# TensorE matmuls into an unused bank during the scatters and the norms of the expert stages

## The chip, the core and the metric

The kernel is one program on one NeuronCore of a Trainium2 chip. The core has a matrix engine (TensorE, PE in the rows), a vector engine (VectorE, DVE), a scalar engine (ScalarE, ACT), a general engine (GpSimd, POOL) and SyncE (SP), which here only starts DMA transfers. Each engine works through its own instructions in order, and they signal each other with semaphores. The metric is the device time of one execution in microseconds, the median over several runs. TensorE's clock has two levels here, 1.2 GHz and 2.4 GHz; the profile gives the granted clock as a share of the higher one, 0.50 or 1.00 (a mean over the stretch asked for).

## What is computed

Six layers on x of shape (2, 1024, 128), that is N = 2048 tokens of 128 numbers, everything in fp32. The layers are, cut from the reference:

```
x = x + 0.5 * L0_ffn(layernorm(x))    # 8 experts, at most N/8 = 256 tokens each, relu
x = x + L0_attn(layernorm(x))         # gated linear attention, 16 heads of 8, a scan over time
x = x + 0.5 * L0_ffn(layernorm(x))
x = x + 0.5 * L1_ffn(layernorm(x))    # 8 experts, no limit, hidden width 512, gelu
x = x + L1_attn(layernorm(x))         # softmax attention, its own norm inside
x = x + 0.5 * L1_ffn(layernorm(x))
```

An expert layer picks for each token the expert with the largest router logit, runs that expert's two matrices on the token (128 to 128 to 128 in L0, 128 to 512 to 128 in L1), and scales the result with the router's probability.

## The kernel before

Tokens lie in 16 tiles of 128 (T = 16), x stays in SBUF as X. The stages run in the order of the layers, with ln the number of the norm and k that of the expert stage: FFN0 (ln 0, k 0), linear attention (ln 1), FFN0 (ln 2, k 1), FFN1 (ln 3, k 2), softmax attention (ln 4), FFN1 (ln 5, k 3). The work of each engine is written out by hand, one function for each engine, and every dependence is a wait on a semaphore. There is no scheduler.

A norm works in four chunks of four tiles. VectorE adds the result of the stage before to X, one instruction a tile (line 1086, semaphore x_updated), takes statistics, and writes the normed tiles to XN (line 1042, xn_ready). TensorE transposes the four tiles of a chunk into PSUM bank 0 or 1 (line 554), and ScalarE copies them to XNT (line 883). Behind the transposes of chunk c TensorE computes the router's logits of chunk c-1 (line 536, tiny matmuls of 128x8) or, in the linear stage, the gates (line 543), and the last chunk's at the end. VectorE turns the logits into expert numbers and slots, and waits for that on logits_done. After an FFN0 stage the results come back by 16 gathers of GpSimd (line 1409), one a tile; after an FFN1 stage by four loads of SyncE.

An expert stage begins with two small bf16 matmuls that count tokens (lines 568 and 569, PSUM bank 3). When VectorE has the slots, GpSimd writes the 16 tiles to DRAM in slot order by 16 indirect DMAs (line 1395), all of which add to one semaphore, scattered. SyncE waits for all 16 and then loads the slots back (line 453), four tiles a load. TensorE transposes them group by group (turn, line 581), and ScalarE copies the transposed groups (line 894). In FFN0 each of 8 experts has an up matmul (line 593), ScalarE's relu, and two down matmuls (line 601). The third group's transposes stand ahead of the first expert's up. In FFN1 there are 23 tiles; each has four up matmuls (line 629), a bias on VectorE, gelu on ScalarE (line 928) and four down matmuls (line 640), and ScalarE copies each tile's W1 in front (line 917). TensorE's order there is up(0), up(1), down(0), up(2), down(1) and so on.

The other lines that the text names: 678 values of the linear stage; 699 its output projection, 8 matmuls a batch; 722 the q and k projections of softmax attention, 726 its values, 16 matmuls; ScalarE's table load of line 933 stands ahead of the gates' sigmoid. An fp32 matmul shows as two records in the trace; a transpose as one.

Of the kernel before, what the change touches and what calls it, by code (L numbers as in the profile page):

```python
# [16 lines left out]
P = 128  # L17
B, S = 2, 1024
N = B * S
T = N // P  # L20
# [122 lines left out]
def macaron_kernel(nc, x_in, params, f1_pack, f1_b2, out):  # L143
    with ExitStack() as ctx:
# [3 lines left out]
        def sem(name):  # L148
            return ctx.enter_context(nc.semaphore(name))
# [159 lines left out]
        gath_ready = sem("gath_ready")  # L309
        owner_ready = sem("owner_ready")  # L310
        xg_ready = sem("xg_ready")
        scattered = sem("scattered")
        xs_loaded = [sem(f"xs_loaded{k}") for k in range(6)]
        xs_turned = sem("xs_turned")
        xs_copied = sem("xs_copied")
# [9 lines left out]
        x_updated = sem("x_updated")  # L325
# [106 lines left out]
        def _(sp):  # L432
# [14 lines left out]

            def moe(kind, k):

                sp.wait_ge(scattered, 16 * T * (k + 1))  # L450
                for c, (a, b) in enumerate(chunks_of(kind)):
                    width = P if kind == "ffn0" else P + 1
                    sp.dma_start(XS[:, a:b, 0:width], sx_rows[k][:, a:b, :]).then_inc(xs_loaded[c], 16)
                if kind == "ffn0":
                    for e in range(E):

                        sp.wait_ge(eo_copied, before(k, E, NT) + e + 1)
                        sp.dma_start(sy_rows[:, 2 * e:2 * e + 2, :], EO[:, 2 * e:2 * e + 2, :]).then_inc(eo_stored, 16)
                    return

                sp.wait_ge(y_scattered, 16 * NT * (k - 1))
                for c in range(T // 4):
                    sp.dma_start(YG[:, 4 * c:4 * c + 4, :], ty_rows[:, 4 * c:4 * c + 4, :]).then_inc(y_loaded[c], 16)
# [62 lines left out]
        def _(pe):  # L526
            ident = col("ident")

            def norm_turned(ln, kind):

                wr = col("f0_wr" if kind == "ffn0" else "f1_wr")
# [14 lines left out]
                if ln == 5:  # L546

                    pe.wait_ge(z_scaled, GR)
                for c in range(T // 4):
                    pe.wait_ge(xn_ready, T * ln + 4 * c + 4)  # L550
                    if 4 * ln + c >= 2:
                        pe.wait_ge(xt_copied, 4 * ln + c - 1)
                    for t in range(4 * c, 4 * c + 4):
                        i = nc.tensor.transpose(PS[:, c % 2, (t % 4) * P:(t % 4 + 1) * P], XN[:, t, 0:P], ident)  # L554
                    i.then_inc(xt_turned, 1)
                    if kind in ("ffn0", "ffn1") and c >= 1:
                        logits(c - 1)
                    if kind == "lin" and c >= 1:
                        gates(c - 1)
# [5 lines left out]
            def moe(kind, ln, k):  # L565
# [9 lines left out]
                def turn(c):  # L575
                    a, b = chunks[c]
                    pe.wait_ge(xs_loaded[c], 16 * (k + 1 if c < 4 else k - 1))
                    if c >= 2:
                        pe.wait_ge(xs_copied, nb + c - 1)
                    for t in range(a, b):  # L580
                        i = nc.tensor.transpose(PS[:, c % 2, (t - a) * P:(t - a + 1) * P], XS[:, t, 0:P], ident)  # L581
                    i.then_inc(xs_turned, 1)

                base = before(k, E, NT)
                if kind == "ffn0":
# [800 lines left out]
        def _(pool):  # L1386
            def moe(kind, k):
# [4 lines left out]
                for t in range(T):  # L1392
                    if kind == "ffn0":
                        pool.wait_ge(xg_ready, T * k + t + 1)
                    pool.indirect_dma_start(sx[k], bass.IndirectOffsetOnAxis(ap=SCATI[:, t:t + 1], axis=0),  # L1395
                                            src[:, t, :], None, bounds_check=slots - 1, oob_is_err=False
                                            ).then_inc(scattered, 16)
                if kind == "ffn1":

                    for i in range(NT):  # L1400
# [131 lines left out]
```

## Time and profile before

| | us |
|---|---|
| median of 3 runs | 989.38 |
| lowest and highest | 987.41, 995.13 |
| span of the profiled execution | 985.3 |
| TensorE busy in it | 675.3 (69%) |
| VectorE busy | 582.2 (59%) |
| ScalarE busy | 443.7 (45%) |
| GpSimd busy | 302.9 (31%) |
| mean granted TensorE clock | 0.834 |

The span is from the first to the last instruction. The rows of the next section but one come from this execution. A row of the timeline merges like instructions that follow each other: its start, the time to the end of the last, the engine, the line, the operation with its operands, the count, and in brackets how long the engine had been idle before it and what ended that. "SPq" is SyncE's issuing of DMAs. Busy time of TensorE is not work at its peak, since a matmul at half clock is busy for twice as long.

### The profile page before, as it was taken

The page shows a single profiled execution, that of the slowest core. Times are in us where ns is not written, and L with a number is a line of the kernel's source. Part 1 is how long each engine was busy: PE and PEld are TensorE (multiplying, and loading weights), DVE is VectorE, ACT ScalarE, POOL GpSimd, SP SyncE. Part 2 cuts the span into 40 slices and gives each one's busy share as a digit, 9 for nine tenths or more (in the row PEclk, how much of TensorE's full clock was granted, in tenths as well). Part 3 has the DMA queues.
Part 4 walks back from the last instruction along what each step waited for, and adds up shares of the span by engine and source line. Part 5 has one row for each costly group of instructions (what it writes and reads, how often), then busy time and mean ns, then how long its engine had stood idle before and what let it go on. Part 6 is the DMA issues. An engine that isn't in the chain of part 4 may idle for free.

```text
span 985.3 us, 13757 instructions
## 1 busy us (share of the span) xinstructions
PE 675.3 (69%) x4446; PEld 334.1 (34%) x4446; DVE 582.2 (59%) x1035; ACT 443.7 (45%) x836; POOL 302.9 (31%) x679
## 2 busy tenths in 40 slices
PE   4042867332240992579999999999999999840694
PEld 4031322131230991213343423242323433230693
DVE  5216699760450345677878777767977777062243
ACT  2021500011210652405878676766667777720462
POOL 0605154414425341003242323141322323105242
PEclk9996889555655896757999999998999999965697
DMA  9942000002213101560030202030020000000203
GB/s 232 274 144 40 1 1 0 0 9 60 71 17 90 30 27 44 123 147 7 1 50 2 50 1 50 1 48 4 11 40 2 1 2 1 1 1 33 81 26 96
DMA packets 45926, 44.89 MB, mean 46 GB/s; under 512 B 5904, under 2 KB 36316, under 8 KB 45600
## 3 DMA queue, kind: packets, MB, share of 16 engines
q1 hardware_dynamic: 41168, 35.90, 15.6%
q0 software_dynamic: 4544, 7.60, 2.9%
q8 instruction: 37, 0.61, 0.3%
q10 hardware_dynamic: 144, 0.51, 0.2%
q14 instruction: 33, 0.27, 0.1%
HBM read 27.85 MB, written 17.60 MB: 46 GB/s over the span
## 4 chain that ended last, share of the span: by engine, by line
PE 51%; DVE 11%; issue 5%; DMA 5%; POOL 5%; ACT 3%; SPq 1%; POOLq 0%; ACTq 0%; DVEq 0%
PE PS L828 14%; PE PS L795 12%; PE PS L770 11%; PE PS L629 5%; PE PS L640 4%; POOL slots_x L1395 3%; DVE ARENA L1348 3%; ACT ARENA L987 2%; DMA ARENA<-slots_x 1%; POOL ARENA L1409 1%; DVE XN L1042 1%; PE PS L536 1%; DMA ARENA<-k_parts 1%; DVE STATS L1019 1%; DVE X L1086 1%
## 5 line engine op out<-in xcount | busy, mean ns | idle before, releaser
L1348 DVE TENSOR_REDUCE ARENA<-PS 128x1 f32<-128x1024 f32 x256 | 302.9, 1219 | 94.6 <-PE PS L770 94.1
L987 ACT ACTIVATE ARENA<-PS 128x512 f32<-128x512 f32 x512 | 279.6, 597 | 95.6 <-PE PS L795 89.2
L795 PE MATMUL PS<-ARENA 75*128 75x512 bf16 x512 | 174.9, 388 | 8.3 <-ACT ARENA L987 6.8
L770 PE MATMUL PS<-ARENA 72*128 72x512 bf16 x512 | 164.3, 406 | 21.3 <-DMA ARENA<-k_parts 16.9
L828 PE MATMUL PS<-ARENA 128*8 128x128 f32 (+8 forms) x1920 | 153.4, 435 | 0.7 <-ACT ARENA L987 0.7
L1460 POOL TENSOR_SCALAR_AFFINE_SELECT ARENA<-ARENA 128x128 f32<-128x128 f32 x256 | 74.6, 296 | 160.5 <-ACT ARENA L987 160.3
L581 PE MATMUL PS<-C,ARENA 128*128 128x128 f32 x78 | 17.1, 368 | 119.5 <-DMA ARENA<-slots_x 119.5
L1272 DVE TENSOR_TENSOR ARENA<-PS,ARENA 128x512 f32<-128x512 f32 x46 | 31.8, 692 | 96.3 <-PE PS L629 96.3
L554 PE MATMUL PS<-C,XN 128*128 128x128 f32 x96 | 24.1, 401 | 92.4 <-DVE XN L1042 88.8
L795 PEld LDWEIGHTS PS<-ARENA 75*128 75x128 bf16 x512 | 47.5, 98 | 105.5 <-ACT ARENA L987 56.5
L770 PEld LDWEIGHTS PS<-ARENA 72*128 72x128 bf16 x512 | 44.8, 100 | 104.1 <-issue 37.3
L894 ACT COPY ARENA<-PS 128x512 f32<-128x512 f32 (+1 forms) x20 | 11.5, 573 | 133.5 <-PE PS L581 133.5
L828 PEld LDWEIGHTS PS<-ARENA 128*32 128x32 f32 (+2 forms) x1920 | 43.7, 98 | 76.0 <-issue 38.7
L1402 POOL DMA_INDIRECT tokens_y<-ARENA x46 | 44.7, 972 | 75.3 <-DVE ARENA L1281 74.3
L1450 POOL CAST ARENA<-ARENA 128x4 bf16<-128x4 f32 x64 | 12.1, 190 | 174.6 <-DVE ARENA L1348 174.5
L1420 POOL TENSOR_TENSOR ARENA<-ARENA 128x1024 f32<-128x1024 f32 x16 | 40.3, 2522 | 55.4 <-DVE ARENA L1318 55.4
L629 PE MATMUL PS<-ARENA 128*128 128x128 f32 x368 | 53.6, 293 | 1.2 <-ACT ARENA L917 0.6
L581 PEld LDWEIGHTS PS<-C,ARENA 128*128 128x128 f32 x78 | 12.2, 188 | 122.8 <-issue 119.2
L640 PE MATMUL PS<-ARENA 128*128 x368 | 51.6, 284 | 1.5 <-ACT ARENA L928 1.5
L1318 DVE TENSOR_TENSOR_SCAN ARENA<-ARENA 128x1024 f32<-128x1024 f32 x16 | 51.8, 3245 | 0.0
L1395 POOL DMA_INDIRECT slots_x<-ARENA,SCATI x32 | 31.4, 983 | 64.5 <-DVE ARENA L1222 56.0
L678 PE MATMUL PS<-XNT,C 128*128 128x512 f32 x64 | 37.3, 725 | 18.2 <-DVE ARENA L1304 18.2
(130 smaller groups left out, 785.0 us busy)
## 6 DMA issues: line engine op xcount, KB each, us to landing
ARENA<-q_parts SPq DMA_DIRECT2D x24, 192.0 KB
ARENA<-k_parts SPq DMA_DIRECT2D x72, 64.0 KB
ARENA<-pack_dram SPq DMA_DIRECT2D x8, 514.0 KB
slots_x<-FILL SPq DMA_DIRECT2D x2, 1483.5 KB, 19.0
ARENA<-slots_x SPq DMA_DIRECT2D x10, 258.0 KB, 4.4
ARENA<-slots_x SPq DMA_DIRECT2D x8, 256.0 KB, 3.6
slots_y<-ARENA SPq DMA_DIRECT2D x16, 128.0 KB, 1.8
ARENA<-tokens_y SPq DMA_DIRECT2D x8, 256.0 KB, 3.7
```

Of the source, the lines that this page charges most:

```text
L629: ins = nc.tensor.matmul(PS[:, 4 + i % 2, f * P:(f + 1) * P], W1[:, i % 2, f * P:(f + 1) * P], XST[:, i * P:(i + 1) * P], start=True, stop ...
L640: ins = nc.tensor.matmul(o, HG[:, i % 2, f * P:(f + 1) * P], WT[:, bass.ds(owner[i] * WB + F1 + f * P, P)], start=(f == 0), stop=(f == FB ...
L770: ins = nc.tensor.matmul(PS[:, slot + c, :], Q3[0:KQ, G % Q3R, g, i * P:(i + 1) * P], K3[0:KQ, G % Q3R, g, c * 512:(c + 1) * 512], start=T ...
L795: nc.tensor.matmul(PS[:, bank, 0:w], K3[0:MR + 3, G % Q3R, i, j * P:(j + 1) * P], Q3[0:MR + 3, G % Q3R, i, half * 512:half * 512 + w], sta ...
L828: ins = nc.tensor.matmul(PS[32 * g:32 * g + width, 7, lo:hi], v, probs, start=(what == "denominator" and st in (0, TB)), stop=(j == TB - 1 ...
L987: nc.scalar.activation(PT[:, n % NPT, 0:w], PS[:, 4 + ring_number[x] % NBB, 0:w], ACT.Exp).then_inc(b_exp, 1)
L1318: nc.vector.tensor_tensor_scan(ST[:, n % 2, :], GT[:, b * S:(b + 1) * S], KV[:, n % 2, :], 0.0, ALU.mult, ALU.add).then_inc(state_done, 1)
L1348: nc.vector.tensor_reduce(NM[:, k % 4, i:i + 1], PS[:, slot:slot + 2, :].rearrange("p b n -> p (b n)"), AX.X, ALU.max, negate=True).then_i ...
L1395: pool.indirect_dma_start(sx[k], bass.IndirectOffsetOnAxis(ap=SCATI[:, t:t + 1], axis=0), src[:, t, :], None, bounds_check=slots - 1, oob_ ...
L1402: pool.indirect_dma_start(ty, bass.IndirectOffsetOnAxis(ap=XS[:, i, P:P + 1].bitcast(U32), axis=0), EO[:, i, :], None, bounds_check=N - 1, ...
L1420: nc.gpsimd.tensor_tensor(QS[:, n % 8, :], QT[:, b * S:(b + 1) * S], ST[:, n % 2, :], ALU.mult).then_inc(qs_done, 1)
L1460: nc.gpsimd.affine_select(out=MD[:, n % NPT, :], in_=PT[:, n % NPT, diag:diag + P], compare_op=ALU.is_ge, fill=0.0, base=0, pattern=[[-1, P]],
```

## The change

TensorE gets a function, keep_busy(times), that multiplies the identity by itself into PSUM bank 3, columns 0 to 127, and whose result nobody reads. It is called at two kinds of places. In all four expert stages, behind the counting matmuls and ahead of the transposes, TensorE waits for the second, third and fourth quarter of the scatters and runs 14 such matmuls after each. In the norms ln 1, 3 and 4 it waits, for each of the 16 tiles, for the addition to X and runs two; these stand ahead of the chunk's transposes. So that a quarter can be waited for, the 16 scatters of a stage add to four semaphores, four scatters each, and SyncE waits for all four.

```diff
-        scattered = sem("scattered")
+        scattered = [sem(f"scattered{q}") for q in range(4)]
...
-                sp.wait_ge(scattered, 16 * T * (k + 1))
+                for q in range(4):
+                    sp.wait_ge(scattered[q], 4 * 16 * (k + 1))
...
+            def keep_busy(times):
+
+                for _ in range(times):
+                    nc.tensor.matmul(PS[:, 3, 0:P], ident, ident, start=True, stop=True)
+
...
+                moes_done = {1: 1, 3: 2, 4: 3}.get(ln)
                 for c in range(T // 4):
+                    if moes_done:
+                        for t in range(4 * c, 4 * c + 4):
+                            pe.wait_ge(x_updated, T * (moes_done - 1) + t + 1)
+                            keep_busy(2)
                     pe.wait_ge(xn_ready, T * ln + 4 * c + 4)
...
                     i.then_inc(xs_turned, 1)
+
+                for q in range(1, 4):
+                    pe.wait_ge(scattered[q], 4 * 16 * (k + 1))
+                    keep_busy(14)
 
                 base = before(k, E, NT)
...
-                                            ).then_inc(scattered, 16)
+                                            ).then_inc(scattered[t // 4], 16)
```

The change moves the line numbers below it: the transposes of the norm are line 554 before and 565 after, those of the experts' input 581 and 592, the up and down matmuls of FFN0 593 and 601, then 608 and 616; keep_busy's matmul is line 533. TensorE's order at the start of the first FFN0 stage, before, from the counting matmuls to the first expert:

```order
L568 MATMUL PS<-MASKB,TRI 128x128
L569 MATMUL PS<-MASKB,ONES 128x128
L581 MATMUL PS<-C,ARENA 128x128 x12
L593 MATMUL PS<-ARENA,C 128x256 x2
L601 MATMUL PS<-C,ARENA 128x128 x2
```

And now:

```order
L579 MATMUL PS<-MASKB,TRI 128x128
L580 MATMUL PS<-MASKB,ONES 128x128
L533 MATMUL PS<-C 128x128 x42
L592 MATMUL PS<-C,ARENA 128x128 x12
L608 MATMUL PS<-ARENA,C 128x256 x2
L616 MATMUL PS<-C,ARENA 128x128 x2
```

The 42 matmuls (three times 14, with a wait ahead of each 14) stand ahead of all transposes; nothing else has moved. The second place is the norm ahead of the linear attention, from the last down matmuls of FFN0 to the last gates. Before:

```order
L601 MATMUL PS<-C,ARENA 128x128 x4
L554 MATMUL PS<-C,XN 128x128 x8
L543 MATMUL PS<-XNT,C 128x512
L554 MATMUL PS<-C,XN 128x128 x4
L543 MATMUL PS<-XNT,C 128x512
L554 MATMUL PS<-C,XN 128x128 x4
L543 MATMUL PS<-XNT,C 128x512 x2
```

And now:

```order
L616 MATMUL PS<-C,ARENA 128x128 x4
L533 MATMUL PS<-C 128x128 x8
L565 MATMUL PS<-C,XN 128x128 x4
L533 MATMUL PS<-C 128x128 x8
L565 MATMUL PS<-C,XN 128x128 x4
L549 MATMUL PS<-XNT,C 128x512
L533 MATMUL PS<-C 128x128 x8
L565 MATMUL PS<-C,XN 128x128 x4
L549 MATMUL PS<-XNT,C 128x512
L533 MATMUL PS<-C 128x128 x8
L565 MATMUL PS<-C,XN 128x128 x4
L549 MATMUL PS<-XNT,C 128x512 x2
```

Eight added matmuls, two for each tile, stand ahead of each chunk's four transposes; the gates of the chunk before stand where they stood.

## Rows read from the trace of the kernel before

**Rows 1.** Waits: engine, line, who was waited for; us in total, times, longest.

```profile
PE PS L581 <- DMA ARENA<-slots_x: 119.5, 8, 32.2
```

**Rows 2.** Busy time of each engine in three stretches of expert stages, granted clock, DMA.

```profile
240.30:244.70 4.40, 4.10 (x15) 3.36 (x16) 0.00 (x0) 1.91 (x4) 0.00 (x0) 0.50 0.50 132
...
317.40:326.60 9.20, 8.06 (x33) 6.66 (x34) 1.38 (x2) 5.53 (x9) 0.00 (x0) 0.50 0.43 116
327.10:371.40 44.30, 43.20 (x357) 41.03 (x355) 20.95 (x43) 28.24 (x46) 21.09 (x22) 1.00 0.08 26
```

**Rows 3.** Timeline, TensorE: plain fp32 matmuls at half and at full clock.

```profile
193.65 3.64 PE L699 MATMUL PS<-C,ARENA 128*128 128x128 f32 x16 [1.18 <-ACT ARENA L865]
...
402.84 3.73 PE L726 MATMUL PS<-C,XNT 128*128 128x128 f32 x32
```

**Rows 4.** Timeline, second FFN0 stage: the last scatter and SyncE's loads.

```profile
235.47 0.97 POOL L1395 DMA_INDIRECT slots_x<-ARENA,SCATI  x1 [0.30 <-issue]
237.65 2.01 SPq L453 DMA_DIRECT2D ARENA<-slots_x  x4
```

**Rows 5.** Timeline, TensorE: second FFN0 stage from the first transposes.

```profile
240.39 1.95 PE L581 MATMUL PS<-C,ARENA 128*128 128x128 f32 x8 [28.61 <-DMA ARENA<-slots_x]
242.54 1.12 PE L581 MATMUL PS<-C,ARENA 128*128 128x128 f32 x4 [0.21 <-DMA ARENA<-slots_x]
243.45 1.69 PE L593 MATMUL PS<-ARENA,C 128*128 128x256 f32 x4
245.08 0.71 PE L601 MATMUL PS<-C,ARENA 128*128 128x128 f32 x4
245.63 0.60 PE L581 MATMUL PS<-C,ARENA 128*128 128x128 f32 x4
246.06 0.60 PE L593 MATMUL PS<-ARENA,C 128*128 128x256 f32 x2
```

**Rows 6.** Timeline, TensorE and ScalarE: start of the first FFN1 stage's experts.

```profile
321.86 3.76 PE L629 MATMUL PS<-ARENA 128*128 128x128 f32 x16 [0.58 <-ACT ARENA L917]
...
322.88 1.28 ACT L928 ACT_TABLE_LOAD   x1
...
324.79 0.63 ACT L928 ACTIVATE ARENA<-ARENA 128x512 f32<-128x512 f32 x1 [0.62 <-DVE ARENA L1272]
325.44 0.62 ACT L917 COPY ARENA<-ARENA 128x512 f32 x1
325.58 1.68 PE L640 MATMUL PS<-ARENA 128*128 x8
...
327.09 1.06 PE L629 MATMUL PS<-ARENA 128*128 128x128 f32 x8
```

**Rows 7.** Timeline, TensorE: the softmax stage's norm (two chunks) and projections.

```profile
386.95 1.11 PE L554 MATMUL PS<-C,XN 128*128 128x128 f32 x4 [2.33 <-DVE XN L1042]
390.40 2.35 PE L554 MATMUL PS<-C,XN 128*128 128x128 f32 x8 [2.34 <-DVE XN L1042]
393.43 9.58 PE L722 MATMUL PS<-XNT,C 128*128 128x512 f32 x16 [0.68 <-ACT XNT L883]
```

**Rows 8.** Timeline, TensorE: values of the linear stage after two short gaps.

```profile
118.00 3.33 PE L678 MATMUL PS<-XNT,C 128*128 128x512 f32 x4 [1.87 <-DVE ARENA L1304]
122.94 1.98 PE L678 MATMUL PS<-XNT,C 128*128 128x512 f32 x4 [1.61 <-DVE ARENA L1304]
```

**Rows 9.** Timeline: ScalarE in the linear stage's norm; then the norm of FFN1.

```profile
99.91 1.28 ACT L933 ACT_TABLE_LOAD   x1
...
271.02 1.12 PE L554 MATMUL PS<-C,XN 128*128 128x128 f32 x4 [4.90 <-DVE XN L1042]
...
281.52 1.11 PE L554 MATMUL PS<-C,XN 128*128 128x128 f32 x4 [2.68 <-DVE XN L1042]
282.43 3.42 PE L536 MATMUL PS<-C,XNT 128*128 128x8 f32 x16
...
285.89 0.29 DVE L1183 COPY LG<-PS 128x128 f32<-128x128 f32 x1 [4.42 <-PE PS L536]
```

## The prediction

> **What bounds the kernel now.** I read the waits first. TensorE's longest waits that no other engine works through are the ones for the experts' input: 119.5 us over 8 waits, up to 32.2 us each, at the transposes of line 581, which wait for the loads from slots_x [rows 1]. There is one long one in each of the four expert stages. The transposes of the norms (line 554) wait too, for VectorE's XN (line 1042), as the rows of the norms show further down. TensorE can shorten neither wait. What the clock view adds is what happens behind them: TensorE comes back at half clock. From 240.3 to 244.7 us it is busy 4.10 of 4.40 us at 0.50, from 317.4 to 326.6 it is busy 8.06 of 9.20 at 0.50, and only then, from 327.1 to 371.4, does it run at 1.00, busy 43.20 of 44.30 us [rows 2]. 0.50 is 1.2 GHz and 1.00 is 2.4 GHz. In that last stretch TensorE is the bound, so time lost at its beginning is lost at its end.
>
> So the question has three parts: how much of the slow work lies on the path, whether the added matmuls hold the clock up when it matters, and whether they are themselves in the way. TensorE takes its work in order, so every added matmul stands ahead of the transposes that all others wait for.
>
> **The price of an added matmul.** They are plain fp32 128x128 matmuls with both operands in C. The trace has the same shape twice: 8 matmuls of line 699 are 16 records in 3.64 us at half clock, and 16 of line 726 are 32 records in 3.73 us at full clock [rows 3]. One costs 3.64/8 = 0.455 us slow and 3.73/16 = 0.233 us fast. A burst of 14 is 6.4 or 3.3 us, a pair 0.9 or 0.47 us. The change adds 4 x 3 x 14 = 168 and 3 x 16 x 2 = 96 of them.
>
> **The bursts behind the scatters.** GpSimd issues a scatter every 1.28 us (0.97, and 0.30 idle [rows 4]), so quarters are 5.1 us apart. The last scatter of the second FFN0 stage is issued at 235.47, SyncE starts the loads at 237.65, and the first data is used at 240.39 [rows 4, 5]. So the last quarter lands near 237.6, quarter 2 near 232.5, quarter 1 near 227.4, and TensorE has 2.8 us between the last quarter and the data. The first burst starts slow. Plain fp32 matmuls at half clock got the full clock back after some 4.8 us (from 321.86 to about 326.6 [rows 2, 6]) and 5.0 us (the projections from 393.43 on [rows 7]). A slow burst lasts 6.4 us, longer than the 5.1 us between quarters, so the first burst and the start of the second are one unbroken run, and the clock should be up before the second ends. The third then starts at full clock after a gap of at most 2 us and takes 3.3 us: it ends near 240.9, 0.5 us after the data. Does the clock outlast such a gap? The linear stage shows both: the same four records take 1.98 us after a gap of 1.61 us and 3.33 us after one of 1.87 us [rows 8]. I take it as holding three times in four. Where it falls, a part of the third burst is slow and it ends up to 6.4 - 2.8 = 3.6 us after the data.
>
> *The gain, FFN0 stages (2).* The third group of transposes starts at 242.54, when its load lands, and the first expert's matmul at 243.45: 0.91 us, where four transposes at full clock take 0.43 (245.63 to 246.06) [rows 5]. That is 0.48. From the first expert's up matmul to its down matmul it is 1.63 us (243.45 to 245.08), with half a microsecond of ScalarE in it; the up matmul is 0.43 of that quicker. 0.9 us a stage at most, 1.8 in both; from 245.08 on the stage runs at full clock anyway. Half a microsecond of lateness of the first transposes is covered here, since the third group waits for its DMA until 242.54.
>
> *The gain, FFN1 stages (2).* Sixteen records of line 629 take 3.72 us (321.86 to 325.58) and eight of line 640 take 1.51 (to 327.09) [rows 6]; at full clock eight records take 0.93 (a quarter of 3.73 [rows 3]), so 5.23 would be 2.7. With 0.45 from the transposes ahead, TensorE alone would gain 2.9. But ScalarE stands beside it: it loads a table for 1.28 us at 322.88, its gelu follows at 324.79, and its copy of the third tile's W1 at 325.44 [rows 6]. With the chain 0.45 us sooner, the first up starts at 321.4, its bias is ready before the table (now in at 323.7), gelu takes 0.65 to 324.35, the first down 0.93, and the third up starts near 325.35, 1.7 us sooner than 327.09. If the copy alone held it, it would be 325.0, 2.1 sooner. I take 1.8, 3.6 in both stages.
>
> *The cost.* 0.5 us for each FFN1 stage, whose chain starts at the first transposes (1.0), and for one burst in four partly slow, some 1.6 us over four stages. Net for the bursts: 1.8 + 3.6 - 1.0 - 1.6 = 2.8 us. Bounds: a gain of 1.8 + 4.2 = 6.0, and a loss, under the rivals.
>
> **The pairs in the norms.** Before the FFN1 norm's last logits, line 554 takes 1.11 us and line 536 3.42 us, up to 285.85, and VectorE starts at 285.89 [rows 9]: all of it slow, and on the path apart from one half of the logits that hides ScalarE's copy. At full clock 0.45 of the transposes and 1.7 of the logits go: 2.1 us at most. TensorE has room: a chunk takes about 5.2 to 6 us (271.02 to 281.52 is two), and holds 8 x 0.455 + 0.9 + 1.7 = 6.2 us of work slow, 3.1 fast. Slow, it is 0 to 2 us late at the last chunk, but then it has been busy all the time with plain matmuls, which is what raised the clock in [rows 6]. I take three quarters of 2.1: 1.6 us.
>
> The norm ahead of the linear attention has no logits, and ScalarE's copy, its table load at 99.91 and its gates come behind the transposes [rows 9], so only the 0.45 of the transposes counts: 0.3 us. The norm ahead of softmax attention has chunks only 3.45 us apart (386.95 to 390.40 [rows 7]), and at half clock 8 x 0.455 + 0.9 = 4.5 us of work in each: TensorE falls behind until the clock is up, and I take its last transposes as 1 us late. Against that, the last transposes (0.45) and the first projection (two of the sixteen records, 1.7 us slow, 0.85 fast) are quicker; the others hide behind VectorE. 1.3 - 1.0 = 0.3 us.
>
> *A rule weighed.* After a wait four transposes take 1.11 us and in the full-clock stretch 0.60 (245.63) [rows 5, 9], so they follow the clock. The Trainium skill, "TensorE: Matmul & The Clock Gate", Part 4, says that the full clock does not engage for the transpose mode. By that the sum would be about 2.5 us in place of the 5.0 below. No part of the sum goes by it.
>
> The semaphores: SyncE waits for four in place of one, and for the same last scatter; SyncE has nothing else to do there, so this is nothing, at most a tenth or two of a microsecond a stage. PSUM bank 3, which the added matmuls write, is read only for the counts, which is over before the scatters start.
>
> **The sum.** 2.8 + 1.6 + 0.3 + 0.3 = 5.0 us. The profiled execution's span is 985.3, so 980.3; the median of the runs shown, 989.38, is 4.1 above the span, so 984.4 us. That is 0.5% and less than the 1% (9.9 us) that a measurement of this kernel can tell from no change; its three runs spread over 7.7 us.
>
> **The rivals.**
> *The gain is eaten (no net change).* The third burst is slow in several stages, the pairs find the wrong moment, and lateness of 1 to 3 us a stage meets gains of 1 to 2. For it speaks the 3.33 us row [rows 8] and that the 2.8 us between scatter and data is less than even a fast burst. It gives 987 to 991.
> *Slower: the clock does not come up for these bursts.* Then three slow bursts are 19.2 us from 227.4: to 246.6, 6.2 us after the data, in each of four stages 25 us; the norm ahead of softmax adds some 5 and that of FFN1 2: 1021 us. It passes +1% once the third burst is slow in full in about three of the four stages (3.6 us each). Against it: matmuls of the same type did raise the clock [rows 2, 6, 7].
> *All of it works.* Every term at its bound: 1.8 + 4.2 + 2.1 + 0.45 + 1.3 = 9.9 us, 979.5. Only this reaches 1%.
> *The transposes take 1.11 us for four at either clock.* Then 0.48 goes in each FFN0 stage, 0.45 in each FFN1 stage, and part of 0.45 in each of three norms, and the sum is about 2.5 us: 987. The 0.60 of the full-clock stretch speaks against it [rows 5]. This is the rule of the Trainium skill's "TensorE: Matmul & The Clock Gate", Part 4, named above.
>
> **How the numbers follow.** The forecast (a gain of 3 to 8 us) has 0.64, the eaten gain 0.18, slower 0.08, all at its bound 0.08, transposes at one price 0.02. The range goes from the bound of the gain to the eaten gain's end: 979 to 991; what is left out is mainly the slower rival and the scatter of the median. Faster by over 1%: 0.07, within 1%: 0.85, slower by over 1%: 0.08.
>
> **What the changed profile would show.** Right: granted clock 1.00 at the first transposes of all four expert stages; the first transposes within 0.6 us of where the data lands; line 629's first sixteen records in 1.9 us in place of 3.7; 14 matmuls of a third burst in 3.3 us. In the FFN1 norm, the last logits in 1.7. Wrong: third bursts of over 4 us, transposes that no longer wait for a DMA but follow the burst by more than 1 us, and a softmax norm whose transposes run behind XN by several microseconds.

## The result, and the profile after

The changed kernel took 994.35 us (median of 12 runs, 989.06 to 997.30), the kernel before 987.39 us beside it (12 runs, 985.03 to 995.13). The ratio is 1.0056, with a 95% interval of 1.0034 to 1.0078: some 5.5 us slower, where I had forecast 5 us faster. All ratios here are estimated over the fast runs (one slow one, 999.69 us in the first comparison, is left out) and are not the quotient of the medians, which would be 1.0070 for this one. The result is inside the 1% that I called no change, but outside the range that I gave. The profiled execution is the slowest of the 12 (997.30 us); its span is 995.6 us, 10.3 more than before, so the differences read from it are on the large side.

The page after, its first two parts:

```profile
span 995.6 us, 14821 instructions
...
PE 746.5 (75%) x4974; PEld 403.2 (41%) x4974; DVE 582.3 (58%) x1035; ACT 442.6 (44%) x836; POOL 301.4 (30%) x679
...
PEclk9996978657766997856999999998979999965998
```

The mean granted clock is 0.865 where it was 0.834. So the change did what it says to the clock. The waits of TensorE after it, the answer to [rows 1]:

```profile
PE PS L533 <- DMA slots_x<-ARENA,SCATI: 38.6, 3, 21.2
PE PS L533 <- DMA slots_x<-XN,SCATI: 33.3, 4, 15.7
...
PE PS L592 <- DMA ARENA<-slots_x: 4.4, 9, 1.3
```

The transposes (line 592 now, 581 before) wait 4.4 us in place of 119.5, longest 1.3. Most of the rest is now waited for ahead of the bursts, at line 533. The windows of the same stretches as in [rows 2], moved to where they lie now:

```profile
241.00:246.00 5.00, 3.73 (x31) 3.56 (x32) 0.00 (x0) 0.00 (x0) 0.00 (x0) 1.00 0.54 156
323.70:334.00 10.30, 7.97 (x63) 7.10 (x64) 1.38 (x2) 5.75 (x9) 0.00 (x0) 1.00 0.56 148
334.00:378.00 44.00, 42.82 (x352) 40.52 (x351) 20.96 (x43) 27.27 (x46) 20.36 (x21) 1.00 0.08 25
```

Both starts now have 1.00 where they had 0.50. Then TensorE's timeline of the second FFN0 stage, which answers to [rows 5]:

```profile
231.06 8.46 PE L533 MATMUL PS<-C 128*128 128x128 f32 x56 [15.68 <-DMA slots_x<-ARENA,SCATI]
241.26 3.39 PE L533 MATMUL PS<-C 128*128 128x128 f32 x28 [1.74 <-DMA slots_x<-ARENA,SCATI]
245.67 0.63 PE L592 MATMUL PS<-C,ARENA 128*128 128x128 f32 x4 [1.01 <-DMA ARENA<-slots_x]
...
247.88 1.03 PE L608 MATMUL PS<-ARENA,C 128*128 128x256 f32 x4
249.09 0.71 PE L616 MATMUL PS<-C,ARENA 128*128 128x128 f32 x4 [0.18 <-ACT ARENA L921]
```

The two first bursts are one run of 8.46 us, the third takes 3.39 us after a gap of 1.74 us, and the first transposes take 0.63. All of this is as predicted. But they still wait 1.01 us for their load, behind a burst that was over. One start is not as predicted. In the first FFN0 stage the three bursts are one run up to 57.6 us and the transposes wait 1.25 us more for their load, 4.84 us after its issue. The granted clock is 1.00 at the first transposes, but falls to 0.50 at 60.63 and stays there until 64.04:

```profile
58.87 1.43 PE L592 MATMUL PS<-C,ARENA 128*128 128x128 f32 x8 [1.25 <-DMA ARENA<-slots_x]
60.51 1.05 PE L592 MATMUL PS<-C,ARENA 128*128 128x128 f32 x4 [0.21 <-DMA ARENA<-slots_x]
61.35 1.91 PE L608 MATMUL PS<-ARENA,C 128*128 128x256 f32 x4
```

Before, the first expert's four records there took 1.40 us. And of the first FFN1 stage, which answers to [rows 6]:

```profile
330.11 2.02 PE L644 MATMUL PS<-ARENA 128*128 128x128 f32 x16 [0.74 <-ACT ARENA L932]
333.22 1.15 PE L655 MATMUL PS<-ARENA 128*128 x8 [1.08 <-ACT ARENA L943]
334.39 1.13 PE L644 MATMUL PS<-ARENA 128*128 128x128 f32 x8
```

Sixteen records take 2.02 us where they took 3.76, and ScalarE's gelu (line 943) is what the first down matmuls wait for, as the prediction has it.

Where did the time go, then? Each stage is measured here from its first to its last row (the count matmul to the start of the last down matmul for an expert stage; for a norm, from the last down matmul before it to the first work behind it). In us, against before:

| stage | before | after | difference |
|---|---|---|---|
| FFN0 stages, first and second | 44.13, 40.69 | 46.28, 41.10 | +2.15, +0.41 |
| FFN1 stages, first and second | 82.87, 81.70 | 81.72, 81.51 | -1.15, -0.19 |
| y of the first FFN0 stage, norm, up to the linear stage's values | 40.76 | 43.05 | +2.29 |
| y of the second FFN0 stage, norm of FFN1, up to its counts | 36.21 | 40.88 | +4.67 |
| linear stage; norm behind it | 88.12; 14.26 | 86.54; 14.93 | -1.57; +0.67 |
| last part of the softmax stage | 441.52 | 444.25 | +2.74 |

Seven of the ten microseconds are in the two norms behind GpSimd's gathers. (The 2.15 us of the first FFN0 stage are not the bursts' alone: a later trace without bursts has 2.0 us there, with its first transposes 4.54 us after the load's issue. The linear stage is 1.5 to 2.0 us shorter than before in eight traces and within 0.2 us of it in the eleven others, and the changed kernel is twice in each group, so its -1.57 is chance.) ScalarE's rows of the first of them, after:

```profile
84.57 0.58 ACT L898 COPY XNT<-PS 128x512 f32<-128x512 f32 x1 [2.60 <-issue]
87.36 0.30 ACT L873 ACTIVATE RSTD<-MV,EPS 128x4 f32<-128x4 f32 x1 [2.21 <-issue]
96.39 0.58 ACT L898 COPY XNT<-PS 128x512 f32<-128x512 f32 x1 [8.73 <-remote]
96.87 0.30 ACT L873 ACTIVATE RSTD<-MV,EPS 128x4 f32<-128x4 f32 x1
99.74 0.58 ACT L898 COPY XNT<-PS 128x512 f32<-128x512 f32 x1 [2.57 <-PE PS L565]
```

TensorE's rows beside them, and GpSimd's last gather:

```profile
89.09 0.66 PE L565 MATMUL PS<-C,XN 128*128 128x128 f32 x4 [1.15 <-issue]
89.59 1.02 PE L549 MATMUL PS<-XNT,C 128*128 128x512 f32 x2
90.45 2.34 PE L533 MATMUL PS<-C 128*128 128x128 f32 x16
98.59 1.11 PE L565 MATMUL PS<-C,XN 128*128 128x128 f32 x4 [5.80 <-DVE XN L1057]
...
93.47 1.00 POOL L1424 DMA_INDIRECT ARENA<-slots_y,GATHI  x1 [0.30 <-issue]
```

The transposes of the second chunk start at 89.09 and end at 89.75. ScalarE's copy of them, which by the program waits for nothing but their semaphore, starts at 96.39: 7.3 us after their start. ("Remote" in its row means that the profile finds no instruction that ended just before the signal.) I call this the lag; undisturbed it is 0.6 to 1.15 us. The semaphore's own update is in the trace at 96.37, so ScalarE was not slow to see it; and TensorE's next signal, that of the gates matmul which ended at 90.61, has its update at 96.41. Both were held. ScalarE is idle all that time, and TensorE is done with its added matmuls at 92.79 and idle too. Behind the copy in ScalarE's queue stands the square root of the next chunk (line 873), then VectorE's reciprocal and XN, then the transposes at 98.59. In the norm of FFN1 the same happens with 7.33 us (274.69 to 282.02). In the norm ahead of softmax, behind which nothing is gathered, there is no lag.

### The profile page after: what moved, and what is told of

Same layout as the page of the kernel before. It is cut to its first block, busy times and chain, and to the rows that moved or that the text cites. A ratio compares the mean times of both kernels' runs of the same rounds, so it can differ in the third digit from the quotient of the medians.

```text
span 995.6 us, 14821 instructions
## 1 busy us (share of the span) xinstructions
PE 746.5 (75%) x4974; PEld 403.2 (41%) x4974; DVE 582.3 (58%) x1035; ACT 442.6 (44%) x836; POOL 301.4 (30%) x679
## 4 chain that ended last, share of the span: by engine, by line
PE 49%; issue 10%; DVE 10%; DMA 5%; ACT 4%; POOL 3%; SPq 1%; ACTq 0%; DVEq 0%; POOLq 0%
PE PS L843 14%; PE PS L810 12%; PE PS L785 11%; PE PS L655 4%; PE PS L644 4%; DVE ARENA L1363 3%; POOL slots_x L1410 2%; ACT ARENA L1002 2%; DMA ARENA<-slots_x 1%; DMA ARENA<-k_parts 1%; DVE STATS L1034 1%; PE PS L798 1%; PE PS L542 1%; DVE XN L1057 1%; DVE X L1101 1%
## 5 line engine op out<-in xcount | busy, mean ns | idle before, releaser
L533 PE MATMUL PS<-C 128*128 128x128 f32 x528 | 87.3, 334 | 92.7 <-DMA slots_x<-ARENA,SCATI 38.6
L533 PEld LDWEIGHTS PS<-C 128*128 128x128 f32 x528 | 82.0, 244 | 99.1 <-DMA slots_x<-ARENA,SCATI 39.4
L565 PE MATMUL PS<-C,XN 128*128 128x128 f32 x96 | 21.6, 368 | 47.0 <-DVE XN L1057 43.2
L644 PE MATMUL PS<-ARENA 128*128 128x128 f32 x368 | 50.0, 279 | 2.2 <-ACT ARENA L932 1.3
L1410 POOL DMA_INDIRECT slots_x<-XN,SCATI x32 | 31.2, 976 | 65.0 <-DVE SCATI L1257 55.8
```

Of the source, the lines that this page charges most:

```text
L533: nc.tensor.matmul(PS[:, 3, 0:P], ident, ident, start=True, stop=True)
L644: ins = nc.tensor.matmul(PS[:, 4 + i % 2, f * P:(f + 1) * P], W1[:, i % 2, f * P:(f + 1) * P], XST[:, i * P:(i + 1) * P], start=True, stop ...
```

## The experiments

All ratios are to the kernel before, run on the same chip beside it. **Kernels under one heading ran on one chip.** The lags are those of the second chunk in the norm ahead of the linear stage (N1) and in FFN1's first norm (N3), in the profiled execution.

### First comparison: the change, and its parts alone

Theory S: the lag is the loss, and it comes from the small matmuls beside the gathers. Rivals: the bursts delay the loads (D), or the lag was one chance event (N).

The changed kernel again, with no edit:

> The changed kernel again, timed beside the others. Ratio to before about 1.006 (5 to 7 us more). Theory S (late signal): in the norms ahead of the linear attention and of the first FFN1, ScalarE's copy of the second chunk starts about 6 us after TensorE's transposes of it have ended, as in the profile of the change (96.39 against 89.75, and 282.02 against 275.35), and this costs 3 to 5 us at each of the two places. Theory N (a chance event of one execution): the 6 us gap is at one place or none here, and the ratio is still near 1.006.

Measured: 991.44 us, 1.0032 [1.0006, 1.0058], lags 1.51 and 3.03 us. Of its 12 runs three are from 982 to 984 and eight from 988 to 992.

Bursts only:

```
-                moes_done = {1: 1, 3: 2, 4: 3}.get(ln)
+                moes_done = None
```

> The changed kernel without the pairs in the norms: only the bursts of 14 behind the scatters. Theory S: without the pairs no late signal, each expert stage 0.5 to 2 us quicker, ratio 0.996 to 0.998 (2 to 4 us less than before). Theory D (the bursts delay the loads from slots_x, +2 us in the first expert stage and +1.7 in the second): ratio 1.001 to 1.004, with data later behind the last scatter than before.

Measured: 986.74 us, 1.0011 [0.9993, 1.0029], lags 1.15.

Pairs only:

```
-                for q in range(1, 4):
-                    pe.wait_ge(scattered[q], 4 * 16 * (k + 1))
-                    keep_busy(14)
```

> The changed kernel without the bursts: only the pairs in the three norms. Theory S: the loss is here, ratio 1.005 to 1.009, with the 6 us gap ahead of ScalarE's copy of the second chunk in both norms behind gathers, and none in the norm ahead of softmax. Theory D: ratio 0.997 to 1.000, since the loss sits in the bursts.

Measured: 988.99 us, 1.0038 [1.0016, 1.0061], lags 3.75 and 4.59 us, runs from 984.56 to 995.34. The traced execution is the fastest of these.

All semaphores and waits of the change, without any added matmul (both `keep_busy` calls deleted):

> The changed kernel with all its semaphores and waits but none of the added matmuls. All theories in which the matmuls matter: ratio 1.000 within 0.002. If the split of the scatters' semaphore or the waits of TensorE cost anything, it shows here: above 1.002.

Measured: 987.24 us, 1.0012 [0.9998, 1.0026], lags 1.1. So semaphores and waits cost nothing that shows. The loss comes with the pairs, and the bursts, which should have gained 2.8 us, gain nothing. Theory S had expected lags of 6 us and more loss (1.006 and 1.005 to 1.009), and a gain for the bursts. Their 1.0011 is in the range of D, but not in its way: the two FFN0 stages are 1.3 and 0.5 us shorter than before in this trace, not 2 us longer.

But the two traces with lags here do not show that lags of this size cost anything. N1 and N3 together are 1.0 us (the change) and 1.8 us (pairs only) shorter than before in them. The medians of both kernels lie 3.3 and 4.4 us above their traced executions, so most of the loss is in executions that were not traced; that those had longer lags is a guess.

For the bursts, the trace of the bursts alone shows this in the first FFN1 stage:

```profile
305.85 2.89 PE L533 MATMUL PS<-C 128*128 128x128 f32 x23 [0.27 <-DMA slots_x<-XN,SCATI]
309.18 0.48 PE L533 MATMUL PS<-C 128*128 128x128 f32 x2 [0.43 <-issue]
310.59 0.27 PE L533 MATMUL PS<-C 128*128 128x128 f32 x1 [0.94 <-issue]
311.99 0.39 PE L533 MATMUL PS<-C 128*128 128x128 f32 x2 [1.13 <-issue]
312.80 5.02 PE L533 MATMUL PS<-C 128*128 128x128 f32 x28 [0.42 <-DMA slots_x<-XN,SCATI]
317.66 1.04 PE L592 MATMUL PS<-C,ARENA 128*128 128x128 f32 x8
```

The second burst breaks off for 0.43, 0.94 and 1.13 us with "issue" as the reason: TensorE waited for no semaphore. I read it as having no instructions, since one of its instruction fetches of 16 KB over the DMA engines falls there, at 310.1, and takes 1.5 us. The third burst then starts at half clock, takes 5.02 us, and holds the transposes up until 317.66, 4.8 us behind the loads' issue, where 2.9 us are usual. The bursts bring three such fetches of their own (40 where the kernel before has 37). Four of the five traces with bursts of 14 have such breaks around a fetch in this stage. The fifth, a later trace of the change, has a fetch at 307.3, inside its second burst, and no break: the fetch does not always starve TensorE. This part I then tested by itself.

### Second comparison: the pairs, split

Pairs in the softmax norm only, and pairs in N1 and N3 only (there the new line has `{1: 1, 3: 2}`), both without bursts (the lines that take the bursts out are not shown):

```
-                moes_done = {1: 1, 3: 2, 4: 3}.get(ln)
+                moes_done = {4: 3}.get(ln)
```

> The 32 small matmuls stand only in the norm ahead of the softmax (behind the third expert stage, no gathers of GpSimd in that norm); no bursts. Theory S (TensorE's signal at the end of a chunk's transposes comes late only while matmuls are placed in the norm AND GpSimd's gathers run): lag from the start of a chunk's transposes to ScalarE's copy stays at 1.15 us (half clock) or 0.64 to 0.69 (full clock) in every norm, ratio 0.998 to 1.001, runs as close together as those of the kernel before (some 5 us). Rival (the matmuls cost wherever they stand): ratio 1.001 to 1.003, lag above 1.15 us in this norm.

> The small matmuls stand only in the two norms behind which GpSimd gathers (norms 1 and 3, 2 a tile); no bursts. Theory S: the whole loss of the run with pairs alone, ratio 1.003 to 1.005, runs some 10 us apart, and in the trace a lag of chunk 1's transposes to ScalarE's copy of 2 to 7 us in one norm or both. Rival: ratio 1.001 or less and lags of 1.15 us, with the loss in the softmax norm instead.

Then two variations of the second: one wait a chunk and 8 matmuls behind it in place of four waits with 2, and 4 matmuls a tile in place of 2:

```
-                        for t in range(4 * c, 4 * c + 4):
-                            pe.wait_ge(x_updated, T * (moes_done - 1) + t + 1)
-                            keep_busy(2)
+                        pe.wait_ge(x_updated, T * (moes_done - 1) + 4 * c + 4)
+                        keep_busy(8)
```

> As the run with pairs in norms 1 and 3, but TensorE waits once a chunk, for its last tile, and then runs 8 small matmuls in a row, not 4 times 2. If the waits for single tiles between matmuls make the signal late, the lag is 1.15 us in all chunks and the ratio 0.999 to 1.001; if the matmuls behind the transposes do it, the lag of chunk 1 stays above 1.15 us and the ratio at 1.003 to 1.005.

> As the run with pairs in norms 1 and 3, but 4 small matmuls a tile instead of 2. Theory S with a dose (each matmul behind the transposes can hold the signal): lags of chunk 1 as long or longer, 3 to 10 us, ratio 1.005 to 1.010. If only the presence of a wait and a matmul matters, the ratio is that of 2 a tile, 1.003 to 1.005. If the lag was chance, 1.000 to 1.001.

Measured, in this order: 985.68 us, 0.9982 [0.9960, 1.0004]; 985.26, 0.9988 [0.9960, 1.0016]; 983.96, 0.9966 [0.9945, 0.9988]; 985.16, 0.9983 [0.9959, 1.0007]. There is no lag above 1.15 us in the second chunks, not even with twice the matmuls. Theory S, as I had put it, missed here: matmuls beside gathers are not enough for the lag. Either a third thing in the program was needed (the pairs of the softmax norm), or something outside it.

### Third comparison: pairs and change again, and the best forms

> The run with the pairs in all three norms (no bursts) once more, beside other kernels. It was 1.0038 [1.0016, 1.0061] on an earlier chip, with its signals 3.75 and 4.59 us late in norms 1 and 3; its two halves, each run alone on another chip, were 0.9982 (softmax norm) and 0.9988 (norms 1 and 3) with no late signal. If the late signal is chance or belongs to the chip, and the pairs as such are worth what I predicted, this ratio is 0.996 to 1.000 with lags of 0.6 to 1.15 us; if both halves together cost, it is again 1.002 to 1.006 with lags of 2 us or more.

> The changed kernel once more, on the same chip as the pairs alone. If the loss of 0.3 to 0.6 per cent is the program's, not a chip's, 1.003 to 1.006 with runs spread over 10 us; if it belongs to the chips of the earlier comparisons, 0.996 to 1.001. Minus the ratio of the pairs alone it gives the bursts' part: 0.000 if they gain as much as their instruction fetches cost.

Measured: pairs only 996.37 us, 1.0072 [1.0051, 1.0093] (5 runs), lags 7.34 and 7.42; the change 996.07 us, 1.0083 [1.0057, 1.0110] (6 runs), lags 7.42 and 7.38. Both lost more than any of the cases expected for them.

Wide bursts, no pairs: the same columns with 4 matmuls in place of 14, and with XNT in place of the identity as the data that stream through.

```
+            def keep_busy_wide(times):
+
+                for _ in range(times):
+                    nc.tensor.matmul(PS[:, 3, 0:448], ident, XNT[:, 0:448], start=True, stop=True)
...
-                    keep_busy(14)
+                    keep_busy_wide(4)
```

> Bursts only, no pairs, but each burst is 4 matmuls of 448 columns in place of 14 of 128: the same columns and so the same time on TensorE, with 4 instructions (and weight loads) where there were 14. Theory F (the bursts lose their gain because their instructions are fetched over the DMA engines while scatters and loads run, and TensorE starves meanwhile): 40 fetches become 37, no burst is stretched beyond 4 us, the transposes of both FFN1 stages stand 2.4 to 2.9 us behind the loads' issue, and the ratio is 0.997 to 0.999 against 1.0011 with 14. Rival (the bursts gain nothing that reaches the end): 1.000 to 1.002 again.

Measured: 985.19 us, 0.9967 [0.9951, 0.9983]. Beside kernels that lose 7 us, this one gains 3: its lags are 1.15. The same place in its trace as above (its transposes are line 597):

```profile
300.87 8.91 PE L538 MATMUL PS<-XNT,C 128*128 128x448 f32 x16 [15.65 <-DMA slots_x<-XN,SCATI]
311.01 3.27 PE L538 MATMUL PS<-XNT,C 128*128 128x448 f32 x8 [1.23 <-DMA slots_x<-XN,SCATI]
314.18 0.63 PE L597 MATMUL PS<-C,ARENA 128*128 128x128 f32 x4
```

There is no break, the third burst runs at full clock in 3.27 us, and there are 38 instruction fetches in place of 40.

All parts together: wide bursts, pairs in the softmax norm, and in N1 and N3 the form with 8 a chunk.

> All parts in their best form so far: bursts of 4 matmuls of 448 columns, pairs by tile in the norm ahead of the softmax, and in norms 1 and 3 one wait a chunk with 8 small matmuls behind it. If the parts add (0.998 softmax pairs, 0.9966 eights, 0.998 wide bursts): 0.992 to 0.996, the gain of 5 us that I predicted for the change. If every added matmul also costs something that the parts alone do not show: 0.997 to 1.001.

Measured: 993.34 us, 1.0054 [1.0034, 1.0074], lags 7.47 and 6.46. The first chunks are late here too (2.17 and 3.55 us). The form that had been the best in the second comparison loses here, 5 us, and the parts don't add where the lag is there.

### Fourth comparison: the chip, or the program

> Bursts of 4 matmuls of 448 columns, pairs in the norm ahead of the softmax, nothing in norms 1 and 3, where GpSimd gathers. If the signals held back in norms 1 and 3 are what turns the change into a loss (theory S) and the parts add (0.9967 and 0.9982): 0.994 to 0.997, faster than before and than the changed kernel, no lag above 2 us. If parts that gain alone do not gain together: 0.998 to 1.001.

> Pairs in norms 1 and 3 only, no bursts, once more, now on the same chip as the pairs in all three norms. It was 0.9988 with lags of 0.7 us. If the held-back signal belongs to the chip (or to chance), this kernel and the one with all pairs agree within 0.2 per cent on this chip, both with long lags or both without. If it takes the third norm's pairs too, this one is 0.997 to 1.000 with lags up to 1.15 us while the other is 1.003 to 1.007 with 4 to 7 us.

> Pairs in all three norms, no bursts, the yardstick of this comparison (1.0038 and 1.0072 so far). Up to 370 us its program is the same as that with pairs in norms 1 and 3 only, so theory S with a cause in the chip expects the same lags in both; 1.003 to 1.007 if this chip shows them, 0.997 to 0.999 if not.

The last kernel here has the pairs in all norms with a semaphore of their own that nobody waits for:

```
-                    nc.tensor.matmul(PS[:, 3, 0:P], ident, ident, start=True, stop=True)
+                    i = nc.tensor.matmul(PS[:, 3, 0:P], ident, ident, start=True, stop=True)
+                i.then_inc(busy, 1)
```

> As the pairs in all three norms, but the last matmul of each pair raises a semaphore of its own that nobody waits for. If matmuls without a signal behind the transposes hold the transposes' signal back, the lag is 0.7 to 1.15 us here in every chunk and the ratio 0.996 to 0.999; if the signal is held by something else (the running gathers), the lags and the ratio are those of the kernel with pairs in all three norms.

This was the same chip as in the third comparison. Measured: wide bursts and softmax pairs 985.59 us, 0.9992 [0.9969, 1.0015]; pairs in N1 and N3 985.98, 0.9997 [0.9976, 1.0017]; pairs in all norms 986.58, 1.0001 [0.9983, 1.0020]; with a signal 986.92, 1.0007 [0.9989, 1.0024]. None has a lag. The first of them missed its expectation: had its parts added (0.9967 and 0.9982), it would have been 0.994 to 0.997. The kernel with pairs in all norms is the same program that took 996.37 us on the same chip. ScalarE in N1, first in the third comparison, then in the fourth:

```profile
96.96 0.59 ACT L895 COPY XNT<-PS 128x512 f32<-128x512 f32 x1 [8.87 <-remote]
97.45 0.30 ACT L870 ACTIVATE RSTD<-MV,EPS 128x4 f32<-128x4 f32 x1
```

```profile
87.93 0.59 ACT L895 COPY XNT<-PS 128x512 f32<-128x512 f32 x1 [2.14 <-PE PS L565]
90.70 0.30 ACT L870 ACTIVATE RSTD<-MV,EPS 128x4 f32<-128x4 f32 x1 [2.18 <-DVE MV L1038]
```

So neither the program nor the chip alone decides whether the lag comes. What else differed between the comparisons (where the data lay in memory, say, or what ran beside) is not on record, and I did not test it. Whether a signal on each pair would prevent it stays open, since there was no lag to prevent.

### Fifth comparison: the change without the lag

> The changed kernel a fourth time. Its ratio was 1.0056, 1.0032 and 1.0083, always with at least some lag in norms 1 and 3. Theory S: the loss goes with the lag. If chunk 1's lag is 4 us or more in both norms, 1.005 to 1.009; if all lags are 0.6 to 1.15 us, 0.998 to 1.002 (the pairs alone without lag were 1.0001, the bursts of 14 alone 1.0011). If the ratio is above 1.004 without a lag, the theory falls.

> Bursts of 4 matmuls of 448 columns and pairs in the norm ahead of the softmax only. It was 0.9992 [0.9969, 1.0015] in a comparison without lags; the wide bursts alone were 0.9967. Theory S: nothing stands behind the gathers, so this is 0.995 to 1.000 whatever the changed kernel does beside it, and faster than that by 0.2 per cent (no lag there) to 0.8 per cent (lag there).

Measured: the changed kernel 981.87 us, 0.9975 [0.9958, 0.9992], 12 runs; wide bursts and softmax pairs 983.70 us, 0.9986 [0.9969, 1.0003]. The changed kernel has no lag in this trace:

```profile
84.69 0.30 ACT L873 ACTIVATE RSTD<-MV,EPS 128x4 f32<-128x4 f32 x1 [2.37 <-DVE MV L1041]
87.11 0.59 ACT L898 COPY XNT<-PS 128x512 f32<-128x512 f32 x1 [2.12 <-PE PS L565]
89.91 0.30 ACT L873 ACTIVATE RSTD<-MV,EPS 128x4 f32<-128x4 f32 x1 [2.22 <-DVE MV L1041]
```

The expectation for this run was 0.998 to 1.002 if there was no lag; it came out a little better. The same program gave 0.9975 here and 1.0083 in the third comparison, and the long lag goes with it. The kernels without matmuls behind the gathers hold their place in every comparison (0.9967 to 1.0012), and beside the changed kernel with its lag the wide bursts are 1.1% faster. Of the versions tried they are the one to keep, on one comparison of them alone; with the softmax pairs they were 0.9992 and 0.9986, not told from 1.

### What all twenty traces say together

| lag in N1 and N3 | kernels with small matmuls there | ratios |
|---|---|---|
| 6.5 to 7.5 us | change (2), pairs, all best forms | 1.0056, 1.0083, 1.0072, 1.0054 |
| 1.5 to 4.6 us | change, pairs | 1.0032, 1.0038 |
| up to 1.15 us | change, pairs, pairs with a signal, pairs in N1 and N3 (2), 8 a chunk there, 4 a tile there | 0.9975, 1.0001, 1.0007, 0.9988, 0.9997, 0.9966, 0.9983 |

In the eight long lags (four traces of three programs), ScalarE's copy starts 2.9 to 3.2 us after the issue of the last of the 16 gathers (96.39 after 93.47 in the rows above), about when that gather lands (its last packets end 2.9 to 3.3 us after the issue). The four shorter lags end earlier, from 2.9 us before that issue to 0.2 us behind it. In each of the four traces the stages of N1 and N3 together are 6.4 to 7.4 us longer than before. The second chunk's transposes are never late in a kernel that has no matmuls there (seven traces), though the third chunk of FFN1's norm shows 1.65 to 1.93 us in four of them, one of these the kernel before.

For the four expert stages together, summed as in the table of stages, against before: kernels without bursts -1.5 to +1.5 us, mean -0.3 (10 traces); bursts of 14 matmuls +1.2, +2.2, -2.1, +0.6 and -3.3, mean -0.3 (5 traces); wide bursts -3.5, -2.4, -4.1 and -3.5, mean -3.4 (4 traces). All are differences to one trace of the kernel before. In the expert stages the two burst forms overlap in one case (-3.3, the change without a lag).

## Why the prediction was wrong, step by step

**The clock: right in the main.** Bursts one and two merge, the third runs at full clock after a gap of 1.7 us, the clock is 1.00 at the first transposes, and line 629's first sixteen records (line 644 now) take 2.02 us (1.9 predicted). But two of the 20 expert stages with bursts of 14 fell back to half clock at their first expert: the first FFN0 stage shown above, and the second one of the change in the third comparison, whose data came 1.39 us behind the burst and whose first four up records took 1.88 us. The prediction has no term for this. Four transposes take 0.60 to 0.66 us at full clock and 1.11 at half. The Trainium skill, "TensorE: Matmul & The Clock Gate", Part 4, says that the full clock does not engage for the transpose mode. These rows differ from it, and the measurement decides.

**The gain in the expert stages: right in size, for bursts that I had not costed.** I had 2.8 us net. In the expert stages wide bursts give 3.0 us more than kernels without bursts; in the device time they gained 3.3 us alone and 0.8 and 1.4 with the softmax pairs. Bursts of 14 give nothing on the mean (+2.2 to -3.3). The term that failed is the cost: I priced a burst by TensorE's time alone, at 0.233 or 0.455 us a matmul, and put its instructions at nothing. 528 records (each with a weight load) are four more fetches in the whole kernel, and all fetches behind them move. In the changed kernel one lies at 242.3, and SyncE's loads of that stage take longer to issue than in [rows 4]:

```profile
241.30 3.40 SPq L454 DMA_DIRECT2D ARENA<-slots_x  x4
```

3.40 us in place of 2.01, and the transposes wait 1.01 us for the data. In all four traces of the changed kernel these loads take 2.90 to 3.40 us, and in all other traces 2.01. That a fetch disturbs the bursts and the loads is argued from their times. That the wide form gains is measured; that it does so by its fewer instructions is the likely reading, but its data differ too, and the two forms never ran in one comparison without pairs. My term for one burst in four partly slow (1.6 us) was too dear for the reason that I gave: four of 36 third bursts were slow. Ahead of two of them (5.02 and 5.86 us) TensorE had starved. The other two (5.56 and 4.97 us) had gaps of 1.51 and 1.88 us ahead of them, and the first also a break of 0.28 us; another burst ran at full clock after the same 1.88 us. So the gap that I took as decisive does not decide it alone.

**FFN1's norm: the mechanism right, the sum wrong.** I had 1.6 us. Without a lag the stage of N3 gains 1.25 us on the mean of six traces with matmuls by tile (0.6 to 2.0), against 0.1 us lost in six traces that have none there (8 a chunk behind one wait lost 0.9). The last logits are down from 3.42 to 1.90 us (I had 1.7) in eight of eleven traces with matmuls by tile, but not in the first trace of the change, where they take 3.42 still. With the long lag the stage loses 2.7 to 4.9. **N1** I had at 0.3: without a lag 0.5 with the pairs and 0.4 without them, which is nothing that can be told; with the long lag, 2.3 to 4.5 lost. **The softmax norm** I had at 0.3: 0.1 gained with pairs (12 traces), 0.2 without (7), so nothing.

**What was missing.** The failed step is the sentence "TensorE has room". It counts TensorE's time between two chunks and takes for granted that the signal of the transposes goes out when they end. In its place the trace shows a signal up to 6.8 us behind that end, and ScalarE waits for it: ScalarE, in whose queue the next square root stands behind that copy. None of my rivals had it. "The gain is eaten" gave 987 to 991 by other reasons; "slower" was priced for a clock that doesn't rise, and the clock rose.

**The semaphores: right.** 1.0012 for all waits without matmuls, not told from 1.

**The sum.** In the comparison without a lag the change gains 2.5 us (0.8 to 4.1), half of the 5.0 predicted. In the two whose traces have lags of 7.3 to 7.4 us it loses 5.5 and 8 us. In the one with 1.5 and 3.0 it loses 3 us, which that trace does not explain. One small slip is in the working: two FFN1 terms at full clock are 1.87 + 0.93 = 2.8 us and not 2.7, which changes nothing.

What stays open is what holds TensorE's signal back. At the second chunk it was seen only with small matmuls in a norm beside running gathers, the long form ends when the last gather lands, and in the traces, one execution of each kernel, it comes in some comparisons for all such kernels and in others for none, on the same chip too. The two groups among the runs of the change in the first comparison suggest that it can differ between executions as well. Neither the number of matmuls (2, 4 or 8 at a time) nor the number of waits decides it: 8 behind one wait had no lag once and 7.47 us the other time, there together with bursts and softmax pairs.

## What to carry to other kernels

Count work that is put on an idle engine in instructions too, not in microseconds alone: the same columns in wide matmuls kept the clock up and took 3 us from the expert stages, where many small ones took nothing on the mean. Before work is put behind a signal for which another engine waits, look at what else goes on there (gathers, loads), and at what stands behind the waiting instruction. When a small change gives different answers in two comparisons, repeat it on another chip and another time before its cause is looked for: one comparison of this change would have told either +0.8% or -0.25%, each far outside the other's interval.

## What the runs showed that I had not expected

A signal of TensorE reached ScalarE up to 7.5 us after the transposes had started, in four traces at the same two places.

The last stage moves by chance. From the start of its first group to the last norm, 20 traces with the same instructions there show 440.1 to 447.2 us, and never a value between 441.6 and 443.0. It goes with the clock: over the whole stage the mean granted clock is 0.957 in the shortest (440.1 us) and 0.937 in the longest (447.2 us), and the correlation over the 20 is -0.96. What moves the clock there is not shown. One window of it in three kernels, the granted clock being the last but two of the numbers; first before (441.5 us for the stage), then wide bursts with softmax pairs (446.2 us), then 4 matmuls a tile (447.2 us):

```profile
720.00:740.00 20.00, 19.60 (x147) 6.66 (x147) 14.05 (x16) 12.12 (x25) 4.25 (x19) 0.93 0.14 22
```

```profile
720.00:740.00 20.00, 19.68 (x121) 6.33 (x120) 13.85 (x16) 11.31 (x24) 3.66 (x17) 0.84 0.08 12
```

```profile
720.00:740.00 20.00, 19.68 (x134) 6.56 (x135) 11.92 (x15) 10.21 (x22) 3.95 (x18) 0.78 0.14 21
```

So 2.7 of the 10.3 us by which the profiled spans differ can't be put down to the change.
